# Scaling the queries on GpSimd and reordering TensorE's value and state products

## The reference, cut to what matters

```python
def step(carry, inp):
    c, n, m = carry
    qt, kt, vt, it, ft = inp
    m_t = jnp.maximum(ft + m, it)
    ie = jnp.exp(it - m_t)
    fe = jnp.exp(ft - m_t + m)
    c = fe[:, :, None, None] * c + ie[:, :, None, None] * jnp.einsum('bhd,bhe->bhde', vt, kt)
    n = fe[:, :, None] * n + ie[:, :, None] * kt
    num = jnp.einsum('bhde,bhe->bhd', c, qt)
    den = jnp.maximum(jnp.sum(n * qt, -1, keepdims=True), 1.0)
    return ((c, n, m_t), num / den)
...
h = o * jnp.moveaxis(hs, 0, 1).reshape(Bs, Sl, HID)
hn = _layernorm(h.reshape(Bs, Sl, H, HD), mh_g, mh_b).reshape(Bs, Sl, HID)
out = (hn + x_skip) * jax.nn.silu(r_t)
return out @ W_down.T + b_down + x
```

## Time and profile before

| | |
|---|---|
| median of 3 runs | 448.0 us (445.31 to 449.13) |
| span of the profiled execution, first to last instruction | 448.0 us |
| busy in that span | PE 383.7 us (86%), DVE 342.7 us (77%), ACT 225.4 us (50%), POOL 125.8 us (28%) |
| passes of the attention loop, from `take_r` of chunk 0 to the next | 64.3 us each |
| mean granted TensorE clock | 0.958 |

### The profile page before, as it was taken

One profiled execution on the slowest core, in us unless ns is written; L12 is line 12 of the kernel. 1 busy time (PEld: TensorE's weight loads), 2 busy tenths in 40 slices (PEclk: granted clock), 3 DMA queues, 4 the chain that ended last, 5 costly groups with the idle time before them and its releaser, 6 DMA issues.

```text
span 448.0 us, 11432 instructions
## 1 busy us (share of the span) xinstructions
PE 383.7 (86%) x3623; PEld 302.6 (68%) x3645; DVE 342.7 (77%) x1061; ACT 225.4 (50%) x591; POOL 125.8 (28%) x125
## 2 busy tenths in 40 slices
PE   8166999999998899898899898899888967879991
PEld 5022999945876677776668676678667843669991
DVE  4883577766649989869989689999699997658870
ACT  3731444425465565455584455475555641455650
POOL 5574244511003101111110121111021138544552
PEclk9669899999999999999999999999999987999996
DMA  7996122159999999999500000000000612333320
GB/s 217 368 411 177 39 72 71 54 147 168 168 166 158 169 162 166 153 150 159 102 1 0 0 0 0 0 0 0 1 1 1 233 53 83 108 99 91 88 78 2
DMA packets 57265, 46.11 MB, mean 103 GB/s; under 512 B 4111, under 2 KB 53905, under 8 KB 56721
## 3 DMA queue, kind: packets, MB, share of 16 engines
q1 hardware_dynamic: 53618, 37.84, 41.8%
q0 software_dynamic: 2752, 5.73, 3.7%
q10 hardware_dynamic: 864, 2.15, 1.6%
HBM read 17.99 MB, written 27.25 MB: 101 GB/s over the span
## 4 chain that ended last, share of the span: by engine, by line
issue 41%; PE 23%; DVE 18%; POOL 9%; ACT 3%; DMA 3%; DVEq 1%; POOLq 0%; SPq 0%; another core or an unknown queue 0%; ACTq 0%
PE bank L896 21%; POOL HS L567 5%; POOL slots L519 3%; PE bank L1033 1%; DVE ST L1419 1%; ACT WVT L786 1%; ACT E L795 1%; POOL LA L561 1%; DMA XN<-slots 1%; DVE W1R L2006 1%; DVE OUT L2044 1%; DVE W1R L2008 1%; DVE W1R L2005 1%; DMA QKT<-by_token 1%; DMA slots<-XN,POS 1%
## 5 line engine op out<-in xcount | busy, mean ns | idle before, releaser
L567 POOL TENSOR_TENSOR HS<-HS,MHALF 128x8 f32<-128x8 f32 x16 | 26.3, 1646 | 148.2 <-DVE HS L1999 148.2
L786 ACT ACTIVATE WVT<-bank,AC 128x128 f32<-128x128 f32 x128 | 36.6, 376 | 29.0 <-PE bank L896 29.0
L896 PE MATMUL bank<-XBT,W1R 128*128 128x128 f32 x368 | 50.6, 282 | 0.2 <-ACT XBT L689 0.2
L896 PE MATMUL bank<-W,HT 128*128 x368 | 49.0, 276 | 1.6 <-issue 1.6
L896 PEld LDWEIGHTS bank<-XBT,W1R 128*128 128x128 f32 x368 | 45.8, 196 | 1.0 <-ACT XBT L689 0.6
L896 PEld LDWEIGHTS bank<-W,HT 128*128 128x128 f32 x368 | 44.8, 192 | 2.3 <-issue 2.0
L696 ACT ACTIVATE HT<-bank,W1R 128x128 f32<-128x128 f32 x115 | 34.8, 366 | 16.6 <-PE bank L896 10.9
L896 PE MATMUL bank<-MASKB,IDB 128*128 128x512 bf16 x130 | 35.6, 400 | 4.9 <-POOL HS L567 3.2
L519 POOL DMA_INDIRECT slots<-XN,POS x32 | 32.2, 1006 | 18.7 <-issue 8.7
L750 ACT ACTIVATE QKT<-bank,COLS 128x512 f32<-128x512 f32 x32 | 22.0, 687 | 26.5 <-PE bank L896 26.5
L1953 DVE TENSOR_TENSOR WOT<-bank,WVT 128x512 f32<-128x512 f32 x32 | 21.9, 685 | 14.7 <-ACT WVT L786 14.7
(11 more groups left out here) (360 smaller groups left out, 983.6 us busy)
## 6 DMA issues: line engine op xcount, KB each, us to landing
slots<-FILL SPq DMA_DIRECT2D x74, 258.0 KB
W<-w SPq DMA_DIRECT2D x2, 2048.0 KB, 10.6
XN<-slots SPq DMA_DIRECT2D x23, 129.0 KB
W<-w SPq DMA_DIRECT2D x1, 2064.0 KB
slots<-QKT SPq DMA_DIRECT2D x1, 1483.5 KB, 6.8
XB<-slots SPq DMA_DIRECT2D x23, 64.5 KB
X<-x SPq DMA_DIRECT2D x4, 256.0 KB, 5.3
QKT<-by_token SPq DMA_DIRECT2D x4, 256.0 KB, 4.1
```

What stands on the lines that cost most here:

```text
L567: g.tensor_tensor(HS[:, 3, :], HS[:, 2, :], MHALF[:, 0:H], ALU.pow).then_inc(roots_ready, 1)
L786: ins = a.activation(DT[:, hf, m, :], DM[:, m * P:(m + 1) * P], ACT.Exp, bias=AC[:, c, h:h + 1])
L896: return t_.matmul(o, l, r, start=start, stop=stop, skip_group_check=True)
```

## The change

`scale_q` moves from DVE to POOL. There it stands ahead of `norms` for chunk 0 and behind `roots(c-1)` for chunk c (in the last sequence, ahead of `roots(2)` for chunk 3), and it waits for the scores and for `E1`. On PE `values` comes first and starts the sum in `NB_` (its first product of each half of the heads is no longer split in two, so 14 products instead of 16, that is 28 passes instead of 32), then `from_state`, which adds to it and now signals `hv_full`, then `to_state`. The wait for `NB_` having been read moves from `from_state` to `values`. In the last chunk `early_ranks` stays between the two.

```diff
@@ POOL
+            def scale_q(b, c):
+
+                n = b * NC + c
+                pool.wait_ge(st_full, 2 * n + 2)
+                pool.wait_ge(*dm_read_at(b, f"state{c}"))
+                g.tensor_tensor(QS[:, :, :], QT[:, :, c * P:(c + 1) * P], E1[:, :, :], ALU.mult).then_inc(qs_ready, 1)
+
             def sequence(b, last):
+                scale_q(b, 0)
                 if not last:
                     norms(b + 1)
                 else:
                     rstd(1, 0)
                 roots(b, 0)
+                scale_q(b, 1)
                 roots(b, 1)
+                scale_q(b, 2)
                 if not last:
                     roots(b, 2)
+                    scale_q(b, 3)
                     roots(b, 3)
                     return
+                scale_q(b, 3)
@@ PE, from_state
-                pe.wait_ge(hv_read, n + 1)
                 pe.wait_ge(qs_ready, n + 2)
...
-                            mm(NB_[hf][half, m * 65:(m + 1) * 65], QS[rows, m, half], CS[rows, m, :], m == 0, False)
+                            ins = mm(NB_[hf][half, m * 65:(m + 1) * 65], QS[rows, m, half], CS[rows, m, :], False, True)
+                        if m == 3:
+                            ins.then_inc(hv_full, 1)
@@ PE, values
                 pe.wait_ge(*pj_read_at(b, f"v{c}"))
+                pe.wait_ge(hv_read, b * NC + c + 1)
...
-                        for half in (slice(0, HD), slice(HD, P)):
-                            ins = mm(NB_[hf][half, m * 65:(m + 1) * 65], PT[:, hf, m, half], VX[:, c % 2, 2 * m + hf, :],
-                                     False, True)
-                    ins.then_inc(hv_full, 1)
+                        for half in [slice(0, P)] if m == 0 else [slice(0, HD), slice(HD, P)]:
+                            mm(NB_[hf][half, m * 65:(m + 1) * 65], PT[:, hf, m, half], VX[:, c % 2, 2 * m + hf, :],
+                               m == 0, False)
@@ PE, chunk
+                values(b, c)
+                if last and c == 3:
+                    early_ranks()
                 from_state(b, c)
                 if more:
                     to_state(b, c)
-                if last and c == 3:
-                    early_ranks()
-                values(b, c)
@@ DVE, chunk
                     weigh(b, c, 1)
-                    scale_q(b, c)
```

More of the change, by code:

```diff
@@ L1954, in weigh @@
                                 DT[:, hf, :, :].rearrange("p m t -> p (m t)"), ALU.mult).then_inc(pt_ready, 1)
[L1956 to L1960, removed]
             def new_state(b, c):
@@ L2066, in chunk @@
                     last_gate_scale()
-                    scale_q(b, 3)
                     early_choice()
```

## The result

| | before | after |
|---|---|---|
| median of the runs | 447.43 us (4 runs, 445.31 to 449.13) | 456.5 us (4 runs, 455.4 to 462.82) |
| span of the profiled execution | 448.0 us | 454.5 us |

The changed kernel is slower, by a ratio of 1.0196 (95% interval 1.0147 to 1.0245). Its run of 462.82 us (granted clock 0.941) and, further on, E1's profiled one of 461.15 us (0.940) lie more than 1.5% above the fastest of their kernel and do not count in the ratios. The forecast was 454.0 us, in a range of 447.5 to 460.

The account below looks back on a forecast made before the run. No single engine was taken to bound the kernel: work goes round DVE, ACT, PE and POOL. Three passes at +1.81 (5.4 us) plus 0.6 for the last sequence on 448.0 gave 454.0 us, range 447.5 to 460.

Parts of the forecast that it names:

- slow product: Rival: POOL's product takes 1.57 us, so chunks 1 and 3 lose 0.47 us more each; 458.2 us, chance 0.14.
- chunk 0: First chunk of a pass: POOL's product meets no clash and `take_r` starts earlier; DVE shift -0.09 us.
- The value products, 0.90 us: PE, chunk 2: 28 passes ahead of the state's update, scaled from 1.03 us for 32, delay `new_state` by +0.81 us net.
- chunk 2: Third chunk: `new_state` on DVE waits for PE's value products placed ahead of the update; +0.81 us, cumulative shift +1.26.
- The product on POOL, 1.1 us: POOL's 128x512 `scale_q` multiplication: estimated at 1.1 us, between bounds of 0.52 and 1.57 us.
- chunk 1: Second chunk: `take_r` gains 0.56 us, then `scale_norm` or `norm_products` loses the product's 1.10 us; cumulative shift +0.45.
- The port is held both ways: DVE two-input SBUF instructions and POOL's SBUF-reading product wait for each other; DVE loses all that is left of 1.1 us.
- DVE never waits: Rival: only POOL waits for DVE at the port; +1.4 us a pass, 451.9 us, chance 0.20.
- no clash: Rival: DVE and POOL do not disturb each other; +0.3 us a pass, 448.6 us, chance 0.11.
- Chunk 3: Fourth chunk: POOL's product waits behind `low_xc`, then DVE's `gate_scans` gives way 0.55 us; cumulative shift +1.81.
- the rival on the other side: Rival: value products fill PE's idle time, so `new_state` is not late; 444.5 us, chance 0.08.
- The last sequence: Fourth sequence, behind the loop: no gain in its last chunk, first three between -0.74 and +1.26; taken as +0.6 us.

Follow-up runs that it names:

- E1: Changed kernel with PE's old order and value products in halves, scaling still on POOL: median 455.73 us, ratio 1.0159 to the kernel before.
- E6: Kernel before with only PE's new order, scaling on DVE, all value products in column halves: median 453.04 us, ratio 1.0065 to the kernel before.
- E2: Kernel before with only PE's new order and splitting, scaling left on DVE: median 452.24 us, ratio 1.0126 to the kernel before.
- E3: Changed kernel with all value products in column halves (32 passes): median 454.43 us, ratio 1.0165 to the kernel before.
- E4: Kernel before plus an unused 128x512 product on POOL behind the roots of chunks 0 to 2: median 452.96 us, ratio 1.0157 to the kernel before.
- E5: Kernel before plus an unused 128x512 memset on POOL behind the roots of chunks 0 to 2: median 449.35 us, ratio 0.9980 to the kernel before.

## Why the prediction came out as it did

The sign held, and so did the two mechanisms, the clash of DVE with POOL and the late update of the state; the total was low by 2.5 us. Yet the sum for a pass was +1.81 where +3.47 was measured, little more than half, so the total is nearer than its terms deserve, by luck: 11.6 us on the profiled span of 448.0 would have made 459.6. What closed the gap is the 5.1 us by which that execution was longer outside the passes; the time of a launch, on the other hand, lies some 2 us above its span (456.32 and 454.5 in after's profiled execution, and 1.8 to 3.1 us more in all runs here), and I had added nothing for that. By the number alone the rival "slow product" (458.2 us) lies nearer to 456.5 than my forecast, but its condition, 1.57 us on POOL, is not met: the product took 1.27 to 1.29.

DVE's shift against before, counted from `UB` in both traces. Counted so, the head of chunk 0, where I had foreseen the gain of 0.09, falls in the last row:

| chunk | predicted | measured at | measured | step |
|---|---|---|---|---|
| 0 | -0.09 | `new_state`: 1.28 against 0.87 us behind `UB` | +0.41 | +0.41 (-0.09) |
| 1 | +0.45 | `new_state`: 13.29 against 12.29 | +1.00 | +0.59 (+0.54) |
| 2 | +1.26 | `new_state`: 26.64 against 24.21 | +2.43 | +1.43 (+0.81) |
| 3 | +1.81 | the next `UB` | +3.47 | +1.04 (+0.55) |

- **The value products, 0.90 us.** This is the term that failed. I scaled 1.03 us by 28/32, as if a pass cost the same at any width; they take 1.63. The form was there in the diff, and no row of before showed a wide value product, so it should have had a range. It carries the error in chunk 2 (1.43 against 0.81). It also makes chunk 0 wait: I put nothing there for PE, and `new_state` waits 0.59 us. E6 shows both: in halves, chunk 0 does not wait and chunk 2 waits 0.45 us less than in E2. In the whole change the width is worth 0.86 us up to `low_xc` (E3).
- **The product on POOL, 1.1 us.** 1.27 to 1.29, inside the bounds 0.52 to 1.57. In chunk 1 DVE's lengthening was 1.10 us, since the product began 0.05 before `scale_norm`, and the gain before it was the one predicted (0.60 from +0.41 to -0.19 at `take_r`, 0.56 foreseen). The step holds.
- **The port is held both ways.** I took this from one row and a product that seemed undisturbed; E3 and E4 show it directly. One reading was loose: I called the 0.45 us of the first power the rest of `UB`, but from 199.45 to 200.03 it is 0.58. Every clash here has such a difference, 0.12 to 0.16 us. That DVE waits for POOL is what decided between the forecast and the rivals "DVE never waits" and "no clash".
- **Chunk 3.** I had POOL behind `low_xc` and DVE giving way later for 0.55 us. POOL was ready 0.01 us earlier and DVE waited 1.12 us inside `low_xc`. The value products ahead of it left `from_state` a wait of 0.38 us where I had said 2. The place was right and the winner wrong: in the pass of E3 shown above, in which DVE is first, as I had assumed, this stretch costs 0.43 us (0.55 foreseen), the 0.47 us of `gate_scans`, and `from_state` waits 1.92. The other winner is worth 0.65 us a pass.
- **The update of the state.** `new_state` waits for PE in chunk 2 (1.42 us, I had named about 1), so the rival on the other side is out. E6 gives this place alone +1.05 us a pass.
- **The last sequence.** About +1.15 us against +0.6; the stretch of before has its lower granted clock (0.98) near the end, so at one clock the difference would be larger, if anything. Its chunk 1 pays 1.07 us (`norm_products` 1.75 us at 345.14, where 0.68 is normal). In its last chunk `OH` runs 0.76 us instead of 0.26; the freed time went to POOL's product as foreseen.

## What to carry to other kernels

Before work moves from VectorE to GpSimd, list which VectorE instructions with two SBUF inputs, or of the kind of this `tensor_scalar`, will run beside it: each can cost nearly the whole length of the other, and the loss hides in instructions that start on time and end late. Work that fills an engine's wait is only free if nothing urgent stands behind it; here 1.09 us of value products ahead of the state's update cost 1.05 us a pass. On TensorE, keep passes of one width together. And a change that loses as a whole can hold one part that gains: ask place by place which conditions make it lose.

## What the runs showed of the hardware

- The width of the weights: in 4-byte data with 128 rows and 65 moving columns, a half-wide pass took 0.034 us and a wide one 0.114 in a uniform row; four wide ones among 24 half-wide ones made 1.63 to 1.73 us of what is 1.03 to 1.09 in 32 halves. Two half-wide passes for the two column halves start 0.01 us apart, and a change of width costs about 0.14 us. `from_state`, which mixes the same widths with 64 rows but changes only once, took 0.88 us for 28 passes.
- The second instruction is longer by the rest of the first less 0.12 to 0.16 us: `low_xc` in the changed kernel by 1.12 of 1.26 us, POOL's product in E3 by 1.07 of 1.23, DVE's second in E4 by 0.48 of 0.63.
- Where both start within 0.01 us, either engine can be first, and the winner differs from pass to pass of one run (E3).
- A GpSimd memset of 128x512 (0.53 us) and VectorE's `low_xc` beside it (1.23 us) both kept their length (E5).
- A GpSimd power of 8 columns took 1.64 us, and VectorE's product of two SBUF inputs that started inside it, at 207.79, kept its 0.68 us. A GpSimd product of 512 columns lengthened every such neighbour that started well before its end (with 0.05 us left, one kept its 0.68).
- VectorE's `tensor_scalar` of 128x128 in 4-byte data, one SBUF input, took 0.69 us beside that product and 0.22 otherwise (E3, two passes).
